# Where the value products stand in the loop over head quads: first and second head, or second and fourth

## What is computed

```
q, k, v = heads(x @ Wq + bq), heads(ctx @ Wk + bk), heads(ctx @ Wv + bv)   # 4 x 16 heads x 256 x 8
scores  = einsum('bhqd,bhkd->bhqk', q, k) / sqrt(8)
scores  = where(mask == 0, -1e9, scores)
p_attn  = softmax(scores, axis=-1)
x       = x + einsum('bhqk,bhkd->bhqd', p_attn, v).merge_heads() @ Wo + bo
x       = x + experts(layernorm(x))          # router, one-hot choice, two layers
```

## Time and profile before

| | |
|---|---|
| time, median of 3 runs | 245.91 us (245.41 to 246.24) |
| the profiled execution: its time | 246.41 us |
| the profiled execution: span from the first to the last instruction | 244.6 us |
| busy in the span: PE, DVE, ACT, POOL | 192.2, 175.4, 135.1, 112.5 us |
| mean granted TensorE clock | 0.965 of full |

### The profile page before, as it was taken

How to read it: one execution, slowest core, us unless ns; L and a number is a source line. 1 busy time by engine, 2 the same in 40 slices (tenths; PEclk the granted TensorE clock), 3 DMA queues, 4 the chain that set the end, 5 groups by cost and what they waited for, 6 DMA issues and landing times.

```text
span 244.6 us, 4754 instructions
## 1 busy us (share of the span) xinstructions
PE 192.2 (79%) x1750; PEld 135.3 (55%) x1750; DVE 175.4 (72%) x455; ACT 135.1 (55%) x271; POOL 112.5 (46%) x205
## 2 busy tenths in 40 slices
PE   0378865998565768688989979978878896999994
PEld 0268654887332556553333534534546784798883
DVE  4678889899887779778757776886665555749252
ACT  2136755929894558336677667767793347260200
POOL 8131677985496076811787784774030032000000
PEclk9999999999996879997999999999999997999999
DMA  6994040000000000000000000000000000000000
GB/s 177 353 390 203 0 162 15 0 3 0 1 3 0 0 0 3 3 3 3 0 1 4 0 3 1 0 3 0 3 1 3 0 1 3 0 3 21 24 21 21
DMA packets 4461, 8.75 MB, mean 36 GB/s; under 512 B 514, under 2 KB 3026, under 8 KB 4052
## 3 DMA queue, kind: packets, MB, share of 16 engines
q1 hardware_dynamic: 3636, 7.78, 8.7%
q10 hardware_dynamic: 800, 0.63, 0.9%
HBM read 7.89 MB, written 0.52 MB: 34 GB/s over the span
## 4 chain that ended last, share of the span: by engine, by line
PE 32%; DVE 26%; POOL 19%; issue 10%; ACT 9%; DMA 2%; SPq 1%; POOLq 0%; DVEq 0%
PE ps L1364 27%; POOL gate_pt L541 6%; PE ps L1373 4%; POOL w L431 3%; DVE mx L1202 3%; POOL rstd L410 3%; DMA wf<-weights_dram 2%; DVE stats L851 2%; DVE hid_xm L1010 2%; DVE half_c L1192 2%; DVE amax L1085 1%; ACT gate_pt L811 1%; DVE gate_pt L1079 1%; DVE ka_mem L1051 1%; POOL spread L528 1%
## 5 line engine op out<-in xcount | busy, mean ns | idle before, releaser
L1202 DVE TENSOR_REDUCE mx<-ps 128x2 f32<-128x512 f32 x64 | 42.3, 686 | 16.5 <-PE ps L1364 16.4
L811 ACT ACTIVATE gate_pt<-ps 128x512 f32<-128x512 f32 x64 | 37.1, 602 | 15.8 <-PE ps L1364 15.3
L1364 PE MATMUL ps<-w,hid_xm 128*128 128x256 f16 (+1 forms) x288 | 30.3, 263 | 0.5 <-DVE hid_xm L1010 0.5
L541 POOL TENSOR_SCALAR gate_pt<-ka_mem 32x256 f16<-32x256 f16 x64 | 25.6, 401 | 4.4 <-issue 0.2
L1364 PE MATMUL ps<-gate_pt,half_c 128*128 128x512 f16 x64 | 25.0, 393 | 3.2 <-issue 1.8
L1364 PEld LDWEIGHTS ps<-w,hid_xm 128*128 128x128 f16 x288 | 25.4, 101 | 3.7 <-POOL w L423 0.7
L1364 PE MATMUL ps<-qb,gate_pt 128*128 128x256 f16 x128 | 25.5, 282 | 0.8
L1364 PE MATMUL ps<-gate_pt,hid_xm 128*32 128x256 f32 x256 | 20.4, 390 | 1.5 <-ACT gate_pt L811 1.5
L1364 PEld LDWEIGHTS ps<-qb,gate_pt 128*128 128x128 f16 x128 | 9.5, 100 | 18.7 <-issue 11.0
L528 POOL TENSOR_SCALAR spread<-mx 128x16 f16<-128x16 f32 x32 | 5.9, 204 | 24.6 <-DVE mx L1202 18.4
L410 POOL TENSOR_TENSOR rstd<-vareps,halfs 128x2 f32<-128x2 f32 (+1 forms) x19 | 15.9, 838 | 1.6
(11 more groups left out here) (222 smaller groups left out, 503.9 us busy)
## 6 DMA issues: line engine op xcount, KB each, us to landing
stage<-weights_dram SPq DMA_DIRECT2D x2, 1024.0 KB, 11.3
wf<-weights_dram SPq DMA_DIRECT2D x4, 256.0 KB, 8.5
wf<-mask_dram SPq DMA_DIRECT2D x1, 1024.0 KB, 4.8
eb_oT<-ffw_dram SPq DMA_DIRECT2D x1, 768.0 KB, 8.3
ctx_in<-ctx_rows_dram ACTq DMA_DIRECT2D x4, 128.0 KB, 5.5
x_in<-x_dram SPq DMA_DIRECT2D x4, 128.0 KB, 3.1
gate_pt<-ctx_cols_dram SPq DMA_DIRECT2D x1, 512.0 KB, 8.5
out_dram<-ctx_in SPq DMA_DIRECT2D x4, 128.0 KB, 1.7
```

The lines of the kernel that those rows point to most:

```text
L541: ins = nc.gpsimd.tensor_scalar(kz[part, n % KRING, k], ka[part, b, quad], 1.0, 0.0, ALU.mult, ALU.add)
L811: nc_act(pt[:, head % PRING].rearrange("p t n -> p (t n)"), ps[:, 2 + head % 2, :], ACT.Exp, scale=DK ** -0.5).then_inc(sig["probs"], 1)
L1202: V.tensor_reduce(mx[:, b, head:head + 2, t], score_bank(4 * n + i).rearrange("p (h n) -> p h n", h=2), AX.X, ALU.max).then_inc(sig["smax" ...
L1364: return nc.tensor.matmul(dst, lhsT, rhs, start=start, stop=stop, skip_group_check=True)
```

## The change

In the loop body the two value calls for the preceding quad move: from the first and second head (k = 0 and 1) to the second and fourth (k = 1 and 3). Their arguments, waits and signals stay, and so does the code of all other engines. After the loop the two calls for the last quad follow as before.

```
                         if (n, k) in ONEHOT_AT:
                             onehot_columns(*ONEHOT_AT[n, k])
-                        if k < TILES and n >= 1:
-                            weighted_values(n - 1, k)
+                        if k % 2 == 1 and n >= 1:
+                            weighted_values(n - 1, k // 2)
                 for t in range(TILES):
                     weighted_values(B * QUADS - 1, t)
```

## The result

The changed kernel is faster: 243.5 us (median of 4 runs, 242.69 to 244.28) against 246.07 (4 runs, 245.41 to 247.96). The forecast was 243.7. The two medians stand in a ratio of 0.9896. The record's own comparison gives 0.9855, with a 95% interval from 0.981 to 0.990, and does not say how it weights the runs; the ratios further down are of that kind. Either way the gain is clear of nothing and under 2%.

What follows compares the result with a forecast made beforehand. No single bound: PE is busiest, with about 6 us of waits in the loop. Gains of 0.72 + 0.80 + 0.69 = 2.21 take the profiled 246.41 to 244.20; median forecast 243.7, range 242.0 to 245.5.

Steps and rivals of the forecast that it cites:

- The waits at the quad boundary: Between two plain quads PE waits 0.47 for ACT and DVE; the moved second value call, 0.57 long, covers it.
- What is late next is the shift: The shift waits for POOL's spread, with PE's work queued behind it; plain quad from 3.69 to about 3.33.
- the first stretch: Shift at 126.23 to S3 (last scores) of quad 6: 1.17 of waits removed, 0.45 added, gain 0.72.
- The waits in quads 4 and 5: Added waits of the shift for POOL in the two plain quads: 0.13 and 0.32, together 0.45.
- Step 4 holds PE from outside: Tail step at 146.94 and 165.52: a gain counts only if last scores of quads 6 and 10 come earlier, then fully.
- The chain of 7.12: From last scores of quads 6 and 10 through DVE, POOL and ACT to step 4: 7.12, with no value call in it.
- The second stretch: Step 4 at 146.94 to last scores of quad 10: one value call fewer, two half boundaries, less 0.24; gain 0.80.
- The third: Step 4 at 165.52 to loop end: ACT's 0.22 wait goes, two half boundaries give 0.47; gain 0.69, between 0.22 and 0.92.
- The copy of two quads' results: ACT's copy (0.60) starts some 0.2 later in every second quad, at no cost.
- the ring of probabilities: A probabilities buffer comes free later, at quad end; the wait is covered, otherwise costing up to 0.64.
- The clock: No loss entered for PE's step 4 waits, up to 1.7; rival of falls at both: 3.3 lost, 247.0, chance 0.11.
- the rival of a larger gain: The clock fall after 204.20, behind the loop, fails to come, giving 1.64 more: 242.1, chance 0.08.

Runs made afterwards that it cites:

- e1: Against the kernel before, only the first value call moves, so both stand at the second head behind the shift; ratio 0.9997 to the kernel before.
- e2: Against the kernel before, only the second value call moves, to the fourth head; the first stays at the first head; ratio 0.9866 to the kernel before.
- h1: Changed kernel, but up to quad 7 the first value call stays at the first head; ratio 0.9865 to the kernel before.
- e3: Changed kernel, but in quads 6 and 10 the second value call is back at the second head; ratio 0.9929 to the kernel before.
- e4: Kernel before, but in quads 6 and 10 alone the second value call stands at the fourth head; ratio 0.9986 to the kernel before.
- h2: As h1, but in quads 8 and 12 the first value call stands ahead of step 4 of the tail; ratio 0.9824 to the kernel before.
- p1: Changed kernel with POOL's expert-weight splits moved to passes 3, 4, 5, 8 and 9, 12, 13, 14; ratio 0.9795 to the kernel before.

## Why the prediction was right

- The waits at the quad boundary are covered by the second call: shown by the timeline (3.35 against 3.69, forecast 3.33 without and 3.53 with POOL's split) and by e1, which keeps the second call where it was and gains nothing. Of the 0.47 per plain quad only 0.38 was waiting. The other 0.09 is the later start of a value call behind scores (0.31 against 0.22), which the change only takes from S0 to S3.
- What is late next is the shift, with the first call queued behind it: shown in quad 3, where the wait grew from 0.37 to 0.74, by as much as the boundary gave up, and by e2 and h1, where the first call ahead of the shift makes the first stretch 0.75 shorter. The waits in quads 4 and 5 were mis-sized, about zero and 0.11 in place of 0.13 and 0.32, but that in part offsets the 0.09 per quad just named. From the shift of quad 3 to that of quad 5 it is 6.78 (125.57 to 132.35) where the sum had 6.87, since a pass of POOL with a split takes 3.43, not 3.53; this is most of the difference between 0.72 and 0.87.
- Step 4 holds PE from outside, and what leads to it counts fully or nearly so: shown from four sides, by e3 and e4 (a call ahead of the last scores), h2 (a call in the wait) and p1 (POOL's chain). The chain of 7.12 kept its length.
- The second stretch had the right size (0.80 forecast, 0.91 measured). The last scores of quad 8, the shift of quad 9 and step 6 stand in PE's timeline as follows, before and then changed (step 6 at 150.23, above):

```profile
149.88 0.38 PE L1364 MATMUL ps<-gate_pt,half_c 128*128 128x512 f16 x1
...
152.02 0.28 PE L1364 MATMUL ps<-id,spread 128*128 128x128 f16 x2
...
152.44 0.22 PE L1364 MATMUL ps<-id,onehot 128*16 128x128 f16 x1
```

```profile
147.66 0.38 PE L1364 MATMUL ps<-gate_pt,half_c 128*128 128x512 f16 x1
...
149.56 0.28 PE L1364 MATMUL ps<-id,spread 128*128 128x128 f16 x2
```

  The boundary gained 0.24 (2.14 to 1.90), and step 6 took 0.25 of it back (0.42 to 0.67), both as forecast. What was sized too small is the call that no longer stands behind step 4: from step 4 to these scores it is 2.25 instead of 2.94, 0.69 for a call counted at 0.57. I also overlooked that PE would wait for ACT's copy behind step 6 if no call stood there; one does in both orders, so it changes nothing in the sum, and e2 shows what is lost without it.
- The third was mis-sized, 0.69 against 0.89, within its upper bound of 0.92. It was built from two boundaries and ACT's wait. Yet 0.68 is gained as early as step 6 (165.52 to 171.58 before, 163.08 to 168.46 now), ahead of which one value call less stands, as in the second stretch. How much of that lasts to the end of the loop, and how much ACT's 0.22 adds, no run separates.
- The copy of two quads' results and the ring of probabilities cost nothing that the stretches show; neither was tested alone.
- The clock did not fall in the measured part of the loop, in waits of 1.51: from 126 to 184 us the granted clock was 1.00 in all twelve profiles. The Trainium skill's rule (TensorE: Matmul & The Clock Gate, What's actually happening), that recent activity lifts the half rate, took nothing from the gain there. The price of 1.64 in the rival of a larger gain was wrong, as the last section shows; what a fall inside the loop would cost, no run shows.
- The forecast of 243.7 rests on a loop gain of 2.21; the loop gave 2.67, and the median 243.5. With medians that vary by a microsecond between sets of runs, the nearness of the two medians is in part luck and proves less than the stretches do.

## What to carry to other kernels

On an engine that runs in order, work that is ready early and needed late is filler: list the places where the engine waits whatever it does, and put one piece of filler behind each step that feeds another engine and ahead of each step that waits for one; two pieces side by side leave the next place bare. Find the chains that hold the engine from outside, and count what stands ahead of their start, since a piece that moves behind that start is gained there in full or nearly so (0.45 to 0.57 of 0.57 here). When runs vary more than the effect, measure between two events of the trace that every variant has.

## What the runs showed beyond that

The spread from run to run arises mostly ahead of the loop: the first shifted scores of quad 0 stand between 112.07 and 115.20 in the twelve profiles, and the shift of quad 3, an event that nothing in these variants but the first quads touches, between 125.57 and 128.81, 3.2 us apart, while the stretches of the loop repeat to 0.01. Part of it arises in the first quads: from those scores to that shift it takes 12.68 and 12.69 in the two profiles whose granted clock was 1.00 between 112 and 118 us, and 13.21 to 13.81 in the other ten, where it was 0.72 to 0.76. The changed kernel stands in both groups (12.69, and 13.24 when profiled again), so this is not the change.

Behind the loop PE waits 2.83 in all twelve profiles. In the kernel before, the clock fell after it; in the changed one it did not (timeline of PE):

```profile
200.86 0.41 PE L1373 MATMUL ps<-cst,rows 128*128 128x128 f32 x2 [2.83 <-ACT rows L647]
...
201.22 2.78 PE L1364 MATMUL ps<-w,hid_xm 128*128 128x256 f16 x24
205.10 0.29 PE L1364 MATMUL ps<-router,n_mem 128*128 128x8 f16 x6 [1.10 <-DVE n_mem L869]
```

The same wait is followed by full or by half rate. And the 1.64 that I had priced for a fall is not gained when it stays away: the matmuls were done in 2.78 instead of 4.42, and PE then waited 1.10 for DVE. From the last exponential to the end of the span it is 60.91 here and 61.28 before, 0.37 less.
